# Gate products placed behind the first half tile of O's rows, and reciprocals taken for two heads at once, in a cross-attention and mixture-of-experts kernel

## The reference, cut to what matters

```
q, k, v = (layernorm(x) @ wq.T + bq), (ctx @ wk.T + bk), (ctx @ wv.T + bv)
scores = where(mask, q k^T / sqrt(32), -1e9);  probs = softmax(scores)
x2 = x + (probs v) @ wo.T + bo
xn2 = layernorm(x2);  weights, idx = top_k(softmax(xn2 @ w_gate), 2)
out = x2 + sum over the 2 experts of weight * (silu(a) * g) @ c_proj[e],  a, g = split(xn2 @ c_fc[e])
```

## Time and profile before

| what | us |
|---|---|
| median of 3 runs (range) | 2912.38 (2908.65 to 2918.61) |
| the profiled execution's own time | 2922.17 |
| its span | 2920.3 |
| PE busy over the span | 2791.5 (96%) |
| DVE, ACT, POOL busy | 1592.8 (55%), 1374.0 (47%), 1278.3 (44%) |
| attention block | 0 to about 1346 |
| granted clock of TensorE, mean | 0.986 |

### The profile page before, as it was taken

How to read it: one execution, slowest core, us unless ns; L and a number is a source line. 1 busy time by engine, 2 the same in 40 slices (tenths; PEclk the granted TensorE clock), 3 DMA queues, 4 the chain that set the end, 5 groups by cost and what they waited for, 6 DMA issues and landing times.

```text
span 2920.3 us, 53159 instructions
## 1 busy us (share of the span) xinstructions
PE 2791.5 (96%) x17472; PEld 2273.4 (78%) x17472; DVE 1592.8 (55%) x5156; ACT 1374.0 (47%) x3628; POOL 1278.3 (44%) x1920
## 2 busy tenths in 40 slices
PE   6999999999999999967999999999999999999998
PEld 5777777777777777746888888888888888888886
DVE  6888888888888888863333232242332332423331
ACT  5767777667777776743232232232322322323321
POOL 5677777777777776652212121222121212121201
PEclk9999999999999999978999999999999999999999
DMA  4344444444444443425444343434343434343412
GB/s 147 106 119 123 131 124 127 120 109 122 122 129 129 125 124 107 113 81 160 94 87 94 80 102 77 104 76 97 83 91 83 94 85 88 90 89 91 73 32 29
DMA packets 247367, 296.30 MB, mean 101 GB/s; under 512 B 40384, under 2 KB 159168, under 8 KB 245568
## 3 DMA queue, kind: packets, MB, share of 16 engines
q1 hardware_dynamic: 184032, 159.58, 21.1%
q0 software_dynamic: 32768, 67.26, 13.3%
q10 hardware_dynamic: 30304, 66.07, 6.8%
HBM read 125.26 MB, written 67.90 MB: 66 GB/s over the span
## 4 chain that ended last, share of the span: by engine, by line
PE 53%; DMA 1%; issue 0%; ACT 0%; POOL 0%; DVE 0%; SPq 0%; POOLq 0%
PE a_ps L1659 18%; PE g_ps L1659 18%; PE y_ps L1674 18%; DMA fc_raw<-in_c_fc 1%; DMA out<-y,recs 0%; DMA xg<-xn_rows,lists 0%; POOL xg L1452 0%; DMA lists<-table 0%; ACT fc_hi L1515 0%; POOL out L1500 0%; ACT L1555 0%; DVE hidden L1622 0%; ACT y L1571 0%; ACT act_part L1555 0%; SPq L1394 0%
## 5 line engine op out<-in xcount | busy, mean ns | idle before, releaser
L1500 POOL DMA_INDIRECT out<-y,recs x128 | 205.2, 1603 | 1184.3 <-ACT y L1571 863.4
L427 POOL TENSOR_SCALAR probs<-probs,row_inv 128x256 f32<-128x256 f32 x1024 | 506.1, 509 | 298.7 <-DVE row_inv L775 285.0
L1622 DVE TENSOR_TENSOR hidden<-act_part,g_ps 128x512 f32<-128x512 f32 x192 | 132.1, 688 | 893.6 <-ACT act_part L1555 893.6
L570 ACT ACTIVATE probs<-probs,low 128x256 f32<-128x256 f32 x1024 | 511.6, 503 | 193.4 <-DVE low L766 124.8
L766 DVE CUSTOM_DVE_ANT_0 probs<-scores_ps,mask_add,row_any 128x256 f32<-128x256 f32 x1024 | 429.6, 477 | 17.5 <-remote 14.8
L1659 PE MATMUL a_ps<-xe_hi,fc_hi 128*128 128x512 f32 x768 | 300.2, 391 | 4.6 <-DVE xe_lo L1578 2.6
L1674 PE MATMUL y_ps<-pj_hi,ht_hi 128*128 128x512 f32 x768 | 299.5, 390 | 0.7
L1659 PE MATMUL a_ps<-xe_lo,fc_hi 128*128 128x512 f32 x768 | 299.7, 390 | 0.0
L1659 PE MATMUL a_ps<-xe_hi,fc_lo 128*128 128x512 f32 x768 | 299.7, 390 | 0.0
L1674 PE MATMUL y_ps<-pj_hi,ht_lo 128*128 128x512 f32 x768 | 298.9, 389 | 0.0
L1674 PE MATMUL y_ps<-pj_lo,ht_hi 128*128 128x512 f32 x768 | 298.8, 389 | 0.0
(11 more groups left out here) (204 smaller groups left out, 6472.7 us busy)
## 6 DMA issues: line engine op xcount, KB each, us to landing
probs_m<-blocks SPq DMA_DIRECT2D x1024, 64.0 KB
x_quarters<-xg SPq DMA_DIRECT2D x496, 64.0 KB
fc_raw<-in_c_fc SPq DMA_DIRECT2D x24, 1024.0 KB, 5.7
out<-x_xn ACTq DMA_DIRECT2D x32, 512.0 KB, 2.8
xn_rows<-x_xn ACTq DMA_DIRECT2D x32, 512.0 KB
cin<-in_ctx_t ACTq DMA_DIRECT2D x31, 512.0 KB, 6.2
xin<-in_x ACTq DMA_DIRECT2D x31, 512.0 KB, 4.4
quarters<-xn_rows SPq DMA_DIRECT2D x120, 128.0 KB
```

The source lines that it names most:

```text
L427: last = nc.gpsimd.tensor_scalar(probs[:, r, t, :], probs[:, r, t, :], row_inv[:, r, t:t + 1], 1.0, ALU.mult, ALU.mult)
L570: last = nc.scalar.activation(probs[:, r, t, :], probs[:, r, t, :], ACT.Exp, scale=-1.0, bias=low[:, r, t:t + 1], accum_out=row_sum[:, r, ...
L1500: nc.gpsimd.indirect_dma_start(out=out[:, :], out_offset=bass.IndirectOffsetOnAxis(ap=recs[:, i * CT + t, 0:1].bitcast(U32), axis=0), in_= ...
L1622: nc.vector.tensor_tensor(hidden[:, m % 2, :], act_part[:, m % 2, :], g_ps[m % 2][:, :], ALU.mult).then_inc(gated, 1)
```

## The change

Two things. On PE, gate(n-2) moves from before x_turn(n+1, 1) to behind the first half tile of O's rows and the first probs_turn, and gate_sum behind the second half tile. ACT's gate_out moves along, from before the exponents of chunk g+2 to behind those of its head 1. On DVE, `invert` takes two heads in one instruction (128x4 instead of 128x2): it waits until the exponents of the second are there, and frees both for POOL at once. Heads 0 and 1 of a chunk are inverted behind the chunk's four masks, where they stood behind the masks of heads 2 and 3; heads 2 and 3 where head 3's reciprocal stood. In chunk g+2, x2_out of the first tile now goes before logits_out, and heads 2 and 3 follow behind route.

```diff
@@ ACT, step @@
-                    if late:
-                        gate_out(n - 2)
                     for r in range(HPC):
                         if heads:
                             exponents(h + 2 * HPC + r)
+                        if r == 1 and late:
+                            gate_out(n - 2)
@@ DVE @@
                 def invert(g):
                     r = g % RING
-                    dve.wait_ge(exped, g + 1)
-                    nc.vector.reciprocal(row_inv[:, r, :], row_sum[:, r, :]).then_inc(inverted, 1)
+                    dve.wait_ge(exped, g + 2)
+                    nc.vector.reciprocal(row_inv[:, r:r + 2, :], row_sum[:, r:r + 2, :]).then_inc(inverted, 2)
...
                             mask_scores(g * HPC + r)
-                            if r >= 2:
-                                invert(g * HPC + r - 2)
+                        invert(g * HPC)
...
-                    if heads:
-                        invert(g * HPC + 2)
                     if has(n - 3):
                         record(n - 3)
                     if heads:
-                        invert(g * HPC + 3)
+                        invert(g * HPC + 2)
...
+                    if tail:
+                        x2_out(n - 1, 0)
                     if late:
                         logits_out(n - 2)
-                    if tail:
-                        x2_out(n - 1, 0)
+                        route(n - 2)
                     if heads:
                         invert(g * HPC + 2 * HPC + 2)
-                    if late:
-                        route(n - 2)
-                    if heads:
-                        invert(g * HPC + 2 * HPC + 3)
@@ PE, step @@
-                    if late:
-                        gate(n - 2)
                     if proj and n >= 0:
                         x_turn(n + 1, 1)
                     for t in range(TILES):
                         for half in range(HALVES):
+                            if late and t == 0 and half == 1:
+                                gate(n - 2)
                             if tail:
                                 outputs(n - 1, t, half)
-                            if late and t == 0 and half == 0:
+                            if late and t == 0 and half == 1:
                                 gate_sum(n - 2)
```

More of the change, by code:

```diff
@@ L940, in step @@
                         attn_lo(g - 1)
-                    if heads:
-                        invert(g * HPC + HPC + 2)
                     if proj and n >= 0:
@@ L945, in step @@
                     if heads:
-                        invert(g * HPC + HPC + 3)
+                        invert(g * HPC + HPC + 2)
                     if late:
@@ L975, in step @@
                         attn_lo(g + 1)
-                    if heads:
-                        invert(g * HPC + 3 * HPC + 2)
                     if late:
@@ L980, in step @@
                     if heads:
-                        invert(g * HPC + 3 * HPC + 3)
+                        invert(g * HPC + 3 * HPC + 2)
                     if n == LAST:
```

## The result

The changed kernel takes 2981.44 us (median of 4 runs, 2980.33 to 2981.93) against 2912.14 us of the kernel before (median of 4, 2908.65 to 2918.61): a ratio of 1.0226, interval 1.0211 to 1.0242. The span of the profiled execution grew from 2920.3 to 2980.1 us.

What follows compares the result with a forecast made beforehand. A loop through DVE, ACT and POOL was to bound the changed kernel, not PE: +1.75 - 0.5 + 0.2 + 0.3 = +1.75 us on 38.85; 28 x 1.7 = 48 us gave 2959 us, range 2936 to 2974.

Steps and rivals of the forecast that it cites:

- the loop: DVE masks, ACT exponents, DVE inverts, POOL scales, DVE turns and masks again: 40.6 us a step, from 38.85.
- leg 2: From turn(g) to the masked head for probs_turn: 10.3 us in series for 10.8, so -0.5 us a step.
- the gate's wait: PE idle before gate, for DVE's turn of x2: 0.94 us a step goes, at most 30.7 us over the run.
- Leg 1, +1.75: From chunk 0's masks to turn(g), 9.05 us before: head 2's reciprocal now stands behind record, +1.75 us a step.
- Legs 3 and 4: From probs_turn's masked head to turn(g+2), +0.2 us a step; from there to the next masks, +0.3.
- gate_sum's new wait: PE before gate_sum, waiting for gate_parts because gate_out goes behind two exponents on ACT: about 0.45 us a step.
- 28 x 1.7: Added time over the steps with both gate products and record: 48 us, taken as 46 to 48 with the others.
- Faster by the gate's wait: Rival at PE before gate: the wait goes and DVE-ACT-POOL delays hide under PE's work, 2882 to 2895 us; chance 0.12.
- Fewer instructions: Rival at DVE's queue: 256 fewer reciprocals at 0.08 save 20 us with no new wait, 2892 us; chance 0.04.
- A draw: Rival at rstd's root or head 3's scale: delay absorbed, PE's saved wait returns elsewhere, 2905 to 2922 us; chance 0.11.
- 0.5 us a step for bad meetings: Upward allowance: PE and the mask meet worse at outputs, probs_m's transfers start later; 0.5 a step, 14 us more.

Runs made afterwards that it cites:

- the version with the early copy: Kernel before with gate products moved, single reciprocals, and gate_out ahead of head 1's exponents on ACT: 2891.47 us (0.9915), measured again 2898.49 us (0.9943).
- the run with head 2 early: The changed kernel, but in chunk g heads 2 and 3 are inverted singly, head 2 ahead of record: 2947.77 us, 1.0096 of the kernel before.
- the one with the root first: The changed kernel, but POOL runs x's root between heads 1 and 2 of chunk g, pairs kept: 2954.66 us, 1.0125 of the kernel before.
- chunk g+2 single: The changed kernel, but in chunk g+2 heads 2 and 3 are inverted singly, head 2 ahead of route: 2951.94 us, 1.0129 of the kernel before.
- the run with two singles: The changed kernel, but each pair is inverted by two 128x2 instructions back to back, after the second head's exponents: 2971.63 us, 1.0192 of the kernel before.

## Why the prediction was right or wrong

The mechanism was right: the loop sets the step, and both waits came where they were foretold. What failed is the size of the sum, in three of its terms: the wide reciprocal "costed like a 128x2", leg 2 with nothing for a handoff between engines, and the steps ahead of the first gate, counted at nothing.

**The bound, and the loop.** Right. With the gate's wait gone PE could have run a step in 37.9; the version with the early copy does. The pairs made the loop the bound: each edit that took a pair, or what stood behind it, off the loop shortened its own leg and the step.

**Gate products.** Right: the wait before gate went. Alone this gives 11 us (2916.69 to 2905.39), not 30.7. The usual step fell by 0.5 us, from 38.85 to 38.3, some 15 us over 30 steps, and no further: gate_sum waits (the gate move's leg 3 is 8.5 to 8.65, where 7.26 with gate's 0.57 and gate_sum's 0.36 would be 8.19), and the loop takes up the rest. The long steps hide part of what is left.

**Leg 1, +1.75.** Right in its mechanism, with 10.93 for 10.8: the pair's reciprocal came 7.06 us behind the masks (685.01 to 692.07), where 6.92 were costed, and the turn 3.87 behind it, for 3.9. The reciprocal stands idle 0.26 for head 3's exponents, so it is they and not the end of record that release it, and 0.10 of the 7.06 is its own late start. Shown by the run with head 2 early, and by the one with the root first.

**Leg 2, -0.5.** The leg that failed by most. It measured 10.6, not 10.3. Three pieces were too short: ACT's third exponents until xt_hi, 3.15 for 3.0 (699.25 to 702.40); the fourth until the pair's reciprocal, 1.2 for 1.1, of which the wide one's late start is 0.07; and the handoff from DVE's mask to PE's probs_turn, 0.15 for nothing. The others were 0.15 too long together (the turn 2.42 for 2.49, a head's mask 0.85 for 0.9). Ahead of xt_hi ACT pauses: it starts 0.09 to 0.55 us behind the start of the last readout, by the step, where exponents follow a readout after 0.09. What it waits for there is not shown.

**Legs 3 and 4.** 9.63 for 9.58 and 9.98 for 9.95. Right as sums. In leg 3 the scale behind head 3 was worth 0.86 (chunk g+2 single) for 0.94. gate_sum's new wait was there, 0.4 us in 28 weight loads for 0.45, but the early copy gave back only 0.24 of it.

**The sum.** The loop was costed at 40.6 and is 41.1. That is 0.5 x 29 = 15 of the 22 us missed. Of the 0.5, 0.3 is the wide reciprocal, by the run with two singles (steps of 40.8); the rest is leg 2's handoff and xt_hi, less what was costed too long. The other 7 are mostly steps that I didn't count. Steps 0 and 1 have heads, and so pairs, before there is a gate: the masks of step 2 start at 110.28, for 106.09 before and 106.23 in the gate move without pairs, 4.2 us late. The 29th step is another 2. The first and the last gate of the steps, after:

```profile
132.17 0.64 PE L1180 MATMUL attn_ps<-x_xn,wg 128*32 128x256 f32 x8
...
1322.73 0.74 PE L1180 MATMUL attn_ps<-x_xn,wg 128*32 128x256 f32 x8
```

and before:

```profile
124.80 0.64 PE L1189 MATMUL attn_ps<-x_xn,wg 128*32 128x256 f32 x8 [0.96 <-DVE x_xn L723]
...
1261.47 1.08 PE L1189 MATMUL attn_ps<-x_xn,wg 128*32 128x256 f32 x8 [0.95 <-DVE x_xn L723]
```

The first gate is 7.4 us late, of which 4.2 are steps 0 and 1 and the rest its later place in its own step (21.9 us behind the masks, for 18.7). From there on 29 steps take 1190.6 us, against 29 x 38.85 = 1126.7 with the usual step of before. What follows the last gate is 1.4 us shorter (1657.4 for 1658.8). 7.4 + 63.9 - 1.4 is 70, beside the 69 measured. The profiled execution of before took 1136.7 us from gate to gate, with its three long steps, so that the two spans are only 59.8 us apart; its time is 9.8 us above the median. That the other executions of before have fewer long steps fits this, but they have no trace. My 28 x 1.7 should have been 29 x 2.2, and 6 for what lies outside.

**Rivals.** Faster by the gate's wait: its mechanism is real and showed as soon as the pairs were taken out (0.9954); with them it was overrun. Fewer instructions: out, two singles are faster than a pair. A draw: out. **The range** was made from terms of the legs alone; its upper end took in 0.5 us a step for bad meetings, which the wide reciprocal and the handoff used up, and nothing for the steps at the start. That 0.5 was meant for other causes (worse meetings at outputs, later transfers).

The second rule of the Trainium skill cited there ("Perfetto Trace Analysis", section "Optimizing Scalar/DVE Operations": on an engine that isn't full but makes others wait, work may be done sooner when instructions are broken up) is borne out here: by 10 us for the same waits with two instructions, and by 64 us where in two of the pairs the first also goes early. The first, of fewer operations, is not: 256 fewer reciprocals saved nothing.

## What to carry to other kernels

Ask of every value that is produced in pieces who waits for the first piece, and what that waiter does next in its queue: here a 0.08 us instruction, saved, held back a 1 us scaling, a root behind it, and DVE behind the root. Go round the loop of the engines and add it up, with something for each handoff (here 0.03 to 0.10 us from ACT's readout to DVE's reciprocal, 0.15 from DVE's mask to PE), and count the steps from the first one that holds the changed work. Pairs were harmless here where the result had slack, and saved nothing either, since DVE had idle time. And two parts of a change don't add: the gate move was worth 11 us without the pairs and 96 with them.

## What was not expected of the hardware

With pairs alone, PE's waits of 0.38 and 2.6 us around one score were followed by half the granted clock for some 6 us (0.50 from 707.2 to 713, 0.94 from 713 to 715), and that cost 2.8 us a step, about as much as the waits themselves; 1.7 us of repeated work in the gap took 77 us off the run. The kernel before shows the same behind its two longest waits before gate, 1.97 us (the gate at 556.95) and 2.37 us (the gate at 1106.37) in the profiled execution; they are two of its three long steps. A stretch behind each, with the clock third from the end:

```profile
558.50:560.00 1.50, 1.50 (x5) 1.11 (x5) 1.50 (x8) 0.52 (x3) 1.42 (x3) 0.50 0.15 40
...
1106.40:1110.00 3.60, 3.60 (x18) 2.71 (x19) 3.19 (x17) 1.36 (x5) 3.35 (x7) 0.62 0.00 0
```

The Trainium skill, "TensorE: Matmul & The Clock Gate", section "HAM oscillation — how this bites in real kernels", describes the pattern of a wait in each turn of a loop after which the next work starts cold; these rows agree, with 0.50 granted behind the wait. Its example waits for a DMA; here PE waits 2.5 to 3.0 us a step for DVE. In the changed kernel PE is idle for 3.0 us of a step too (41.1 less 38.1), but in waits of 0.3 to 1 us, and the clock stays at 1.00. Most of what the gate move is worth beside the pairs, 96 us (3077 to 2981), is this: filling the wait alone gave 77.

The other surprise is the 128x4 reciprocal, which started 0.10 us behind the end of ACT's readout where a 128x2 one started 0.03 behind it. On a loop with three of them that was 0.3 us a step.
